# Second attention of a two-layer block: transposes by DMA in place of TensorE, rotations merged, the loop unrolled with twelve steps of lag

## The chip, the cores and the metric

One core of one Trainium2 chip (trn2). The metric is the device time of one execution in microseconds: the median of the runs, lower is better.

## The reference, cut to what matters

The kernel computes four stages on `x` (16 batches, 128 rows, 256 columns): a cosine attention, a ternary feed-forward, a rotary attention with grouped heads and a second ternary feed-forward. The change is in the third:

```python
q = (draft_hidden @ Wq.T).reshape(bsz, draft_len, H, HD)
q = _rms_norm(q, q_norm_w).transpose(0, 2, 1, 3)
kv_in = jnp.concatenate([context_hidden, draft_hidden], axis=1)
k = (kv_in @ Wk.T).reshape(bsz, total_len, KVH, HD)
v = (kv_in @ Wv.T).reshape(bsz, total_len, KVH, HD).transpose(0, 2, 1, 3)
k = _rms_norm(k, k_norm_w).transpose(0, 2, 1, 3)
q = _rope(q, draft_position_ids)
k = _rope(k, full_position_ids)
scores = jnp.einsum('bhqd,bhkd->bhqk', q, k) * SCALE
probs = jax.nn.softmax(scores, axis=-1)
attn = jnp.einsum('bhqk,bhkd->bhqd', probs, v)
attn = attn.transpose(0, 2, 1, 3).reshape(bsz, draft_len, H * HD)
return attn @ Wo.T
```

H is 16 heads of HD 128 elements, KVH 4 key and value heads, each repeated for 4 query heads. Its input is the layer norm of `x`, its keys and values come from 128 context rows and the 128 rows themselves, and its result is added to `x`.

## The kernel before

The program has five parts one behind the other, with a barrier of all engines between them: preparation of weights, first attention, first feed-forward, second attention (`part_c`), second feed-forward. The feed-forwards are written out step by step and already transpose their quantised rows by DMA from SP (lines 730 and 736: 2 blocks of 128x128, and 8 or 6 blocks).

`part_c` works in 64 units: for each of the 16 batches four groups of heads, each with 4 query heads and one key and value head over 256 keys. All large products are made of f16 halves: a value is split into a high half and a low half (what is left), and three products of halves are summed in f32 (`PASSES`). A unit passes through stages that lie some steps apart (`PROJ` 3, `ROPE` 4, `TURN` 5, `SCORE` 6, `EXPS` 7, `VALUE` 8, `ATTEND` 9, `OUT` 10). In each step every engine does its share of all stages, each for another unit, in the order in which its function has them; semaphores order the engines among each other. The steps run in a hardware loop of 8, with 3 rounds peeled off.

- PE (TensorE), function `tensor`: transposes of the rotated queries and keys in f32 (lines 1510, 1529), once in four units of y (1520), projection of keys and values (1544) and of queries (1557), transposes of the probabilities in f32 (1569, 1579), output projection (1589), scores (1601), probabilities times values (1613).
- ACT (ScalarE), `scalar`: high halves out of PSUM (1310 attention output, 1316 queries, 1322 keys, 1334 values, 1357 and 1362 probabilities), a copy of the keys (1340) and its scaling (1347), the four exponentials with their sums (1301).
- DVE (VectorE), `vector`: low halves, each the value in PSUM less its high half (1395, 1401, 1408, 1427, 1449, 1466), products of queries with cosine and sine (1384), sums of squares by statistics of each head (1433, 1443) and what combines them (1460 to 1486), the maximum of the scores (1480), the bias of the exponentials (1494), the reciprocal of the sums (1455), the residual (1374).
- POOL (GpSimd), `pool`: reciprocal roots by a power (1242), the rotations of queries (1250) and keys (1259, 1264), the tables (1274), the scaling of the probabilities (1285).
- SP, `sync`: loads of rows, tables and context of a batch into double buffers (1206 to 1210), the residual rows and the store (1216).

## Time and profile before

| | |
|---|---|
| median of 3 runs | 954.79 us (951.28 to 956.22) |
| the profiled execution | 956.97 us, its span 955.3 us |
| busy share of the span | PE 83%, DVE 86%, ACT 63%, POOL 63% |
| PE's mean granted clock | 0.951 of full speed |
| mean rate of the DMA queues | 56 GB/s |

The span is the time from the first to the last instruction of one execution. An engine's busy time leaves out waits on semaphores and the issuing of DMAs. The chain of waits follows, from the end backwards, what each piece of work was released by. A granted clock of 1.00 is 2.4 GHz, 0.50 is 1.2 GHz.

### The profile page before, as it was taken

Reading aid. Unit: us, or ns where it says so; the run is one execution under the profiler, and the core shown is the slowest. Engines: PE = TensorE matmul, PEld = TensorE weight load, DVE = VectorE, ACT = ScalarE, POOL = GpSimd, SP = SyncE. Lnnn points to the kernel's source line nnn. Section 1 sums busy time; section 2 is a strip of 40 time slices with the busy share of each in tenths; the row PEclk is TensorE's granted clock in tenths of the full one; section 3 lists DMA queues with packets and bytes.
Section 4 is the critical chain, followed back from the end, with each engine's and each line's share of the span. In section 5 each row is a group of like instructions: output and inputs, shape, how many; then the busy total and the mean of one; then the engine's idle time right before and its main releaser. Section 6 shows DMA issues by size and latency. Waiting matters only on the chain.

```text
span 955.3 us, 20235 instructions
## 1 busy us (share of the span) xinstructions
PE 791.0 (83%) x5555; PEld 525.2 (55%) x5555; DVE 817.1 (86%) x2370; ACT 600.0 (63%) x1452; POOL 597.6 (63%) x987
## 2 busy tenths in 40 slices
PE   0285988985575679999999999999999999984776
PEld 0152333331233357777777777777777777653443
DVE  7766799865895689999999999999999999854996
ACT  1565778762794267666667776666667776652552
POOL 1500111122563699999999999899899899831453
PEclk9995999997897899999999999999999999998997
DMA  8204355441244000000000000000000000000245
GB/s 297 102 8 130 118 158 156 144 132 39 46 96 96 29 23 7 29 12 19 30 30 1 28 27 22 5 27 27 0 27 27 27 0 11 13 12 11 42 100 120
DMA packets 89272, 53.31 MB, mean 56 GB/s; under 512 B 43988, under 2 KB 88438, under 8 KB 88950
## 3 DMA queue, kind: packets, MB, share of 16 engines
q1 hardware_dynamic: 89206, 52.54, 19.2%
q8 instruction: 28, 0.46, 0.2%
q14 instruction: 38, 0.31, 0.1%
HBM read 22.10 MB, written 6.29 MB: 30 GB/s over the span
## 4 chain that ended last, share of the span: by engine, by line
PE 54%; DVE 17%; issue 11%; ACT 6%; POOL 5%; DMA 3%; SPq 1%; POOLq 1%; DVEq 0%; ACTq 0%
PE psum L1589 8%; PE psum L1613 8%; PE psum L1601 7%; PE psum L1557 7%; PE psum L1544 7%; PE psum L514 3%; PE psum L1569 3%; PE psum L1579 3%; PE psum L1510 2%; DVE arena L829 2%; PE psum L500 1%; ACT arena L811 1%; DMA arena<-arena 1%; DVE arena L917 1%; ACT arena L805 1%
## 5 line engine op out<-in xcount | busy, mean ns | idle before, releaser
L1301 ACT ACTIVATE arena<-psum,arena 128x256 f32<-128x256 f32 x256 | 147.0, 589 | 2.8 <-DVE arena L1494 2.8
L1285 POOL TENSOR_SCALAR arena<-arena 128x256 f32<-128x256 f32 x256 | 124.2, 485 | 38.5 <-DVE arena L1455 17.1
L1310 ACT ACTIVATE arena<-psum 128x512 f16<-128x512 f32 x64 | 38.2, 597 | 161.6 <-PE psum L1613 161.6
L1557 PE MATMUL psum<-wq_t,arena 128*128 128x512 f16 x384 | 94.6, 383 | 5.0 <-DVE arena L1384 4.6
L1589 PE MATMUL psum<-wo_t,arena 128*128 128x256 f16 x768 | 95.6, 275 | 3.0 <-DVE arena L1395 2.8
L1601 PE MATMUL psum<-arena 128*128 128x256 f16 x768 | 94.4, 273 | 2.8 <-ACT arena L1301 2.7
L1544 PE MATMUL psum<-wkv_t,arena 128*128 128x256 f16 x768 | 95.6, 275 | 0.9 <-DVE arena L1421 0.9
L1613 PE MATMUL psum<-arena 128*128 128x512 f16 x384 | 93.3, 379 | 0.0
L1242 POOL TENSOR_TENSOR arena<-arena,minus_half 128x6 f32<-128x6 f32 x64 | 85.2, 1331 | 10.6 <-DVE arena L1486 7.0
L1250 POOL TENSOR_TENSOR arena<-arena 128x256 f32<-128x256 f32 x128 | 90.6, 729 | 0.3 <-DVE arena L1384 0.3
L342 POOL TENSOR_TENSOR arena<-arena 128x256 f32<-128x256 f32 x16 | 12.0, 747 | 119.3 <-DVE arena L421 119.3
L1259 POOL TENSOR_TENSOR arena<-arena 128x256 f32<-128x256 f32 x128 | 79.4, 642 | 9.6 <-ACT arena L1347 8.4
L1384 DVE TENSOR_TENSOR arena<-psum,arena 128x512 f32<-128x512 f32 x128 | 82.0, 680 | 1.1 <-issue 1.1
L1589 PEld LDWEIGHTS psum<-wo_t,arena 128*128 128x128 f16 x768 | 75.5, 99 | 12.7 <-DVE arena L1395 4.2
L1601 PEld LDWEIGHTS psum<-arena 128*128 128x128 f16 x768 | 75.0, 98 | 12.9 <-issue 3.9
L1480 DVE TENSOR_REDUCE arena<-psum 128x4 f32<-128x1024 f32 x64 | 78.1, 1220 | 4.5 <-PE psum L1601 4.0
L1544 PEld LDWEIGHTS psum<-wkv_t,arena 128*128 128x128 f16 x768 | 75.5, 99 | 10.1 <-DVE arena L1421 1.3
L357 ACT ACTIVATE arena<-psum 128x1024 f32<-128x1024 f32 x64 | 65.1, 1019 | 19.6 <-PE psum L483 19.3
L514 PE MATMUL psum<-arena 128*32 128x256 f32 x512 | 71.4, 402 | 1.9 <-ACT arena L357 1.7
L1449 DVE TENSOR_TENSOR arena<-psum,arena 128x512 f16<-128x512 f32 x64 | 44.2, 691 | 23.4 <-ACT arena L1357 21.7
L1264 POOL TENSOR_TENSOR arena<-arena 128x128 f32<-128x128 f32 x128 | 55.7, 457 | 6.5
L1301 ACT ACTIVATION_READ_ACCUMULATOR arena<-psum,arena 128x1 f32 x256 | 59.0, 230 | 0.0
(201 smaller groups left out, 2006.5 us busy)
## 6 DMA issues: line engine op xcount, KB each, us to landing
arena<-split_scratch SPq DMA_DIRECT2D x96, 64.0 KB, 2.7
arena<-in_x SPq DMA_DIRECT2D x32, 128.0 KB, 2.2
split_scratch<-arena SPq DMA_DIRECT2D x32, 128.0 KB, 1.8
x_rows<-arena SPq DMA_DIRECT2D x32, 128.0 KB, 2.0
arena<-x_rows SPq DMA_DIRECT2D x32, 128.0 KB, 2.0
arena<-in_L_ffn_w SPq DMA_DIRECT2D x2, 1024.0 KB, 6.9
x_rows<-in_L_xattn_Wq SPq DMA_DIRECT2D x1, 2048.0 KB, 13.6
ctx_t<-in_L_xattn_Wo SPq DMA_DIRECT2D x1, 2048.0 KB, 11.7
```

Source lines behind the costliest of these rows:

```text
L514: mm = eng.matmul(value_bank(vp)[r:r + 32, half:half + D], v_t[:, vb.lane % 4, k, h, :], probs[:, q, j, k, :], start=(k == 0), stop=(k == 1))
L1242: eng.tensor_tensor(r[:, lane, :], ms[:, t, :], c.minus_half[:, 0:6], ALU.pow).then_inc(S["r"], 1)
L1250: eng.tensor_tensor(q_rot[:, t, :, s, :], q_cos[:, t, :, s, :], q_sin[:, t, :, 1 - s, :], ALU.add)\
L1259: eng.tensor_tensor(to[:, :, :, :], k_n[:, :, :, :], table["k"][:, wb.lane, :, :, :], ALU.mult)\
L1285: eng.tensor_scalar(probs[:, t, h, :], probs[:, t, h, :], share[:, t, h:h + 1], P_SCALE, ALU.mult, ALU.mult).then_inc(S["probs"], 1)
L1301: eng.activation(probs[:, t, h, :], S_BANKS[:, h, :], ACT.Exp, bias=bias[:, t, h:h + 1], scale=r[:, w.lane % 4, h:h + 1], accum_out=total[ ...
L1384: eng.tensor_tensor(to[:, t, :, :, :].rearrange("p h s f -> p h (s f)"), q_view.rearrange("p h s f -> p h (s f)"), table["q"][:, wb.lane, ...
L1544: mm = eng.matmul(KV_BANK[:, KEYS * row:KEYS * row + KEYS], x_t[:, p, s, k, :], c.wkv_t[:, m, k, g, :, :].rearrange("p a d -> p (a d)"), s ...
L1557: mm = eng.matmul(Q_BANK, y_t[:, p, s, k, :], c.wq_t[:, m, k, SHARE * P * g:SHARE * P * g + SHARE * P], start=(n == 0), stop=(n == 5))
L1589: mm = eng.matmul(O_BANK, a_t[:, t, s, P * h:P * h + P], c.wo_t[:, m, SHARE * g + h, :], start=(g == 0 and h == 0 and n == 0), stop=(g == ...
L1601: mm = eng.matmul(S_BANKS[:, h, :], q_t[:, t, s, P * h:P * h + P], k_t[:, t, m, :], start=(n == 0), stop=(n == 2))
L1613: mm = eng.matmul(A_BANK, v[:, w.lane % 8, s, k, :], p_t[:, t, m, k, :], start=(n == 0), stop=(n == 5))
```

## The change

In `part_c` alone (and `norm_cos` and `norm_sin` become two views of one tensor):

- The loop is written out: 76 steps (`STEPS = TOTAL + LAST`), stages at `ROWS` 1, `HALVES` 2, `PROJ` 4, `ROPE` 5, `TURN` 6, `SCORE` 8, `PROBS` 9, `ATTEND` 10, `OUT` 11, `LAST` 12.
- PE transposes nothing. The rotated queries and keys, y, and the probabilities are split into f16 halves in row layout in SBUF, and SP's DMA transposes turn them: one of 12 blocks (queries and keys), two of 8 (high and low half of the probabilities) per unit, one of 4 (y) per batch.
- The low halves are now made from operands in SBUF.
- POOL writes the high half of the probabilities straight from its scaling, as f16, and DVE writes the low half for each of the four heads.
- Sums of squares: six squares with a sum on ACT in place of six statistics and four small instructions on DVE; the reciprocal root is a logarithm and an exponential on ACT in place of a power on POOL.
- The products with cosine and sine are one instruction for both, on DVE (queries) and POOL (keys); the rotated sum of both halves is one instruction with a swapped view; the tables one instead of two.
- The copy of the keys goes; they are scaled out of PSUM. The projections' banks are doubled.
- Rows, context and tables are read where they lie; the loads, the reload of the residual and the store go.

```diff
-    PROJ, ROPE, TURN, SCORE, EXPS, VALUE, ATTEND, OUT = 3, 4, 5, 6, 7, 8, 9, 10
-    LAST = OUT + 1
+    ROWS, HALVES, PROJ, ROPE, TURN, SCORE, PROBS, ATTEND, OUT, LAST = 1, 2, 4, 5, 6, 8, 9, 10, 11, 12
+    STEPS = TOTAL + LAST
...
     def sync(eng):
+        for s in range(STEPS + 1):
+            b = batch(s, HALVES)
...
+                eng.dma_start_transpose(y_t[:, b % 2, :, :, :].rearrange("p s k r -> p (s k) r"),
+                                        y_hl[:, :, :].rearrange("p s n -> p (s n)")).then_inc(y_turned[b % 2], 16)
+            u = unit(s, PROBS)
+            if u is not None:
+                eng.wait_ge(S["p_hi"], SHARE * (u + 1))
+                wait(eng, S["attn"], u - 1)
+                for half in range(2):
+                    if half:
+                        eng.wait_ge(S["p_lo"], u + 1)
+                    eng.dma_start_transpose(p_t[:, u % 2, half, :, :, :].rearrange("p h k r -> p (h k) r"),
+                                            p_hl[:, u % 2, half, :, :].rearrange("p h k -> p (h k)"))\
+                       .then_inc(p_turned[u % 2], 16)
+            u = unit(s, TURN)
+            if u is not None:
+                eng.wait_ge(S["q_lo"], u + 1)
+                eng.wait_ge(S["k_lo"], u + 1)
+                wait(eng, S["scores"], 2 * (u - 1))
+                eng.dma_start_transpose(qk_t[:, u % 2, :, :], qk_hl[:, u % 2, :]).then_inc(qk_turned[u % 2], 16)
     def pool(eng):
...
+                eng.wait_ge(S["q_cs"], u + 1)
+                wait(eng, S["q_lo"], u - 1)
+                eng.tensor_tensor(straight(q_rot[:, u % 2, :, :]), straight(q_cs[:, 0, :, :]), swapped(q_cs[:, 1, :, :]),
+                                  ALU.add).then_inc(S["q_rot"], 1)
...
+                eng.wait_ge(S["k_n"], u + 1)
+                wait(eng, S["k_rot"], u)
+                eng.tensor_tensor(k_cs[:, :, :, :].rearrange("p t n d -> p t (n d)"),
+                                  k_n[:, :, :].rearrange("p n d -> p (n d)").unsqueeze(1).broadcast_to([P, 2, KEYS]),
+                                  turn["k"][:, b % 2, :, :, :].rearrange("p t n d -> p t (n d)"), ALU.mult)\
+                   .then_inc(S["k_cs"], 1)
...
+            u = unit(s, SCORE)
+            if u is not None:
+                eng.wait_ge(S["share"], 2 * (u + 1))
+                wait(eng, p_turned[u % 2], 32 * (u // 2))
                 for h in range(SHARE):
-                    eng.tensor_scalar(probs[:, t, h, :], probs[:, t, h, :], share[:, t, h:h + 1], P_SCALE,
-                                      ALU.mult, ALU.mult).then_inc(S["probs"], 1)
+                    eng.tensor_scalar(p_hl[:, u % 2, 0, h, :], probs[:, u % 2, h, :], share[:, u % 2, h:h + 1], None,
+                                      ALU.mult).then_inc(S["p_hi"], 1)
     def scalar(eng):
...
+            u = unit(s, SCORE)
+            if u is not None:
+                eng.wait_ge(S["bias"], u + 1)
...
+                for h in range(SHARE):
+                    eng.activation(probs[:, u % 2, h, :], S_BANKS[:, h, :], ACT.Exp, bias=bias[:, u % 2, h:h + 1],
+                                   scale=r[:, u % 8, h:h + 1], accum_out=total[:, u % 2, h:h + 1])\
+                       .then_inc(S["exps"], 1)
+            u = unit(s, PROJ)
+            if u is not None:
...
+                for n in range(2):
+                    eng.activation(junk[:, SHARE + n, :], kv_bank(u)[:, n, 0, :], ACT.Square,
+                                   accum_out=sums[:, u % 2, SHARE + n:SHARE + n + 1])
+            u = unit(s, ATTEND)
+            if u is not None:
+                eng.wait_ge(S["attn"], u + 1)
+                wait(eng, S["o"], u - 1)
+                eng.activation(a_t[:, u % 2, 0, :], A_BANK, ACT.Copy, scale=A_SCALE).then_inc(S["a_hi"], 1)
+            u = unit(s, PROJ)
+            if u is not None:
+                eng.wait_ge(S["q_cs"], u + 1)
+                for h in range(SHARE):
+                    last = eng.activation(junk[:, h, :], q_bank(u)[:, P * h:P * h + P], ACT.Square,
+                                          accum_out=sums[:, u % 2, h:h + 1])
+                last.then_inc(S["ss"], 1)
     def vector(eng):
+        for s in range(STEPS + 1):
+            u = unit(s, OUT)
+            if u is not None:
+                eng.wait_ge(S["a_hi"], u + 1)
+                eng.scalar_tensor_tensor(a_t[:, u % 2, 1, :], A_BANK, A_SCALE, a_t[:, u % 2, 0, :], ALU.mult,
+                                         ALU.subtract).then_inc(S["a_lo"], 1)
+            u = unit(s, PROBS)
+            if u is not None:
+                for h in range(SHARE):
+                    eng.wait_ge(S["p_hi"], SHARE * u + h + 1)
+                    last = eng.scalar_tensor_tensor(p_hl[:, u % 2, 1, h, :], probs[:, u % 2, h, :],
+                                                    share[:, u % 2, h:h + 1], p_hl[:, u % 2, 0, h, :],
+                                                    ALU.mult, ALU.subtract)
+                last.then_inc(S["p_lo"], 1)
+            u = unit(s, SCORE)
+            if u is not None:
+                eng.wait_ge(S["scores"], 2 * (u + 1))
+                wait(eng, S["bias"], u - 1)
+                eng.tensor_reduce(top[:, u % 2, :], S_BANKS, AX.X, ALU.max).then_inc(S["top"], 1)
+            u = unit(s, TURN)
+            if u is not None:
+                eng.wait_ge(S["q_hi"], u + 1)
+                eng.tensor_tensor(q_hl(u, 1), q_rot[:, u % 2, :, :].rearrange("p h d -> p (h d)"), q_hl(u, 0),
+                                  ALU.subtract).then_inc(S["q_lo"], 1)
...
+            u = unit(s, PROJ)
+            if u is not None:
...
+                eng.tensor_tensor(
+                    q_cs[:, :, :, :],
+                    q_bank(u).rearrange("p (h d) -> p h d", h=SHARE).unsqueeze(1).broadcast_to([P, 2, SHARE, HEAD_DIM]),
+                    turn["q"][:, b % 2, :, :].unsqueeze(2).broadcast_to([P, 2, SHARE, HEAD_DIM]), ALU.mult)\
+                   .then_inc(S["q_cs"], 1)
```

The order in a step of `scalar` is: high halves of queries and keys (`TURN`), logarithm and exponential of the sums, high half of the values, the two scaled keys (`ROPE`), once per batch what y needs, four exponentials (`SCORE`), two squares of the keys (`PROJ`), the high half of the output (`ATTEND`), four squares of the queries (`PROJ`). That of `vector`: low half of the output (`OUT`), four low halves of the probabilities (`PROBS`), the maximum (`SCORE`), the low half of the queries (`TURN`), the bias (`SCORE`), the low half of the keys (`TURN`), the merged products of the queries (`PROJ`), the residual once per batch, the scaled sums of the exponentials once all four are there (`SCORE`), the low half of the values (`ROPE`), their reciprocal, and once per batch statistics, y and its low half. That of `pool`: query rotation, key products, key rotation (`ROPE`), a table, four scalings (`SCORE`). That of `tensor`: scores, projections, probabilities times values, output projection.

## Rows read from the trace of the kernel before

**Rows 1.** Timeline of SP at the start of the second attention (start us, us).

```profile
307.64 0.52 SPq L1206 DMA_DIRECT2D arena<-x_rows  x1
```

**Rows 2.** Chain of waits (start us, us, what), in order of time.

```profile
314.86 2.74 PE psum L1544 x12
...
396.10 1.42 PE psum L1557 x6
...
501.32 0.44 PE psum L1510 x4
...
501.98 1.31 PE psum L1544 x12
...
505.02 0.44 PE psum L1579 x4
...
792.81 1.38 PE psum L1557 x6
...
871.47 1.96 DMA x_rows<-arena
```

**Rows 3.** Busy us by stretch: length, PE, PEld, DVE, ACT, POOL, clock, DMA share, GB/s.

```profile
400.00:730.80 330.80, 329.78 (x2506) 251.21 (x2504) 318.44 (x904) 228.82 (x690) 301.54 (x512) 1.00 0.06 21
244.40:298.90 54.50, 36.74 (x206) 18.06 (x204) 48.99 (x195) 51.88 (x65) 33.29 (x44) 1.00 0.44 85
299.00:319.40 20.40, 11.30 (x45) 6.29 (x46) 5.52 (x18) 2.33 (x4) 4.89 (x9) 0.50 0.29 78
```

**Rows 4.** Groups by line and form: xcount | busy us, mean ns | idle before.

```profile
L1285 POOL TENSOR_SCALAR arena<-arena 128x256 f32<-128x256 f32 x256 | 124.2, 485 | 38.5 <-DVE arena L1455 17.1
L1250 POOL TENSOR_TENSOR arena<-arena 128x256 f32<-128x256 f32 x128 | 90.6, 729 | 0.3 <-DVE arena L1384 0.3
L1259 POOL TENSOR_TENSOR arena<-arena 128x256 f32<-128x256 f32 x128 | 79.4, 642 | 9.6 <-ACT arena L1347 8.4
L1480 DVE TENSOR_REDUCE arena<-psum 128x4 f32<-128x1024 f32 x64 | 78.1, 1220 | 4.5 <-PE psum L1601 4.0
L1395 DVE SCALAR_TENSOR_TENSOR arena<-psum,arena 128x512 f16<-128x512 f32 x64 | 43.4, 678 | 6.7 <-ACT arena L1310 6.7
L1374 DVE SCALAR_TENSOR_TENSOR arena<-psum,arena 128x256 f32<-128x256 f32 x16 | 6.6, 414 | 1.6 <-PE psum L1589 1.6
```

**Rows 5.** Timeline of ACT: two exponentials and their accumulator reads.

```profile
504.79 0.60 ACT L1301 ACTIVATE arena<-psum,arena 128x256 f32<-128x256 f32 x1
505.24 0.24 ACT L1301 ACTIVATION_READ_ACCUMULATOR arena<-psum,arena 128x1 f32 x1
505.33 0.61 ACT L1301 ACTIVATE arena<-psum,arena 128x256 f32<-128x256 f32 x1
```

**Rows 6.** Timeline in the first feed-forward: a transpose of 8 blocks, and its reader.

```profile
261.28 1.30 SPq L736 DMA_TRANSPOSE arena<-arena  x1
...
264.41 1.05 PE L954 MATMUL psum<-t_b,arena 128*128 128x256 f16 x8 [0.47 <-DMA arena<-arena]
```

**Rows 7.** DMA rate from 261 to 264.5 us in 40 slices of 0.0875 us.

```profile
GB/s 0 0 35 152 222 205 111 23 0 0 1 0 0 0 0 0 0 50 190 228 219 214 222 214 219 205 214 187 219 196 188 170 59 3 0 0 0 0 0 0
```

**Rows 8.** Timeline of DVE and POOL in three places of the kernel.

```profile
106.60 0.68 DVE L450 TENSOR_TENSOR arena<-arena 128x512 f16<-128x512 f32 x1
106.78 1.09 POOL L345 TENSOR_TENSOR arena<-arena 128x256 f32<-128x256 f32 x1
...
150.79 0.73 POOL L345 TENSOR_TENSOR arena<-arena 128x256 f32<-128x256 f32 x1 [1.31 <-DMA arena<-in_x]
150.82 1.25 DVE L466 SCALAR_TENSOR_TENSOR arena<-arena 128x512 f32<-128x512 f32 x1
...
416.72 2.20 POOL L1285 TENSOR_SCALAR arena<-arena 128x256 f32<-128x256 f32 x4
417.18 0.16 DVE L1470 SCALAR_TENSOR_TENSOR arena<-arena 128x12 f32<-128x12 f32 x1
417.37 0.41 DVE L1475 TENSOR_TENSOR arena<-arena 128x6 f32<-128x6 f32 x1
```

**Rows 9.** One line of DVE: duration ns min/median/max, first and last start.

```profile
L1475 DVE TENSOR_TENSOR arena<-arena x64: 166/167/412, 321.3 to 830.1; 128x6 f32<-128x6 f32 x64
```

More of the change, by code:

```diff
@@ L1188, in part_c @@
+    q_head = lambda u, s, h: qk_t[:, u % 2, SHARE * s + h, :]
+    k_keys = lambda u, s: qk_t[:, u % 2, 2 * SHARE + 2 * s:2 * SHARE + 2 * s + 2, :].rearrange("p n k -> p (n k)")
     S = {n: c.sem("c_" + n) for n in (
[L1189 to L1192 removed]
@@ new lines, in part_c, with unit @@
+        "eps", "stats", "rstd", "y", "y_hi", "y_lo", "tables", "q", "kv", "ss", "r", "q_cs", "q_rot", "k_n", "k_cs",
+        "k_rot", "v_hi", "v_lo", "q_hi", "q_lo", "k_hi", "k_lo", "scores", "top", "bias", "exps", "share", "p_hi",
+        "p_lo", "attn", "a_hi", "a_lo", "o", "out")}
+    y_turned = [c.sem(f"c_y_turned{p}") for p in range(2)]
+    qk_turned = [c.sem(f"c_qk_turned{p}") for p in range(2)]
+    p_turned = [c.sem(f"c_p_turned{p}") for p in range(2)]
+    def unit(s, lag):
+        u = s - lag
+        return u if 0 <= u < TOTAL else None
@@ new lines, in batch @@
+    def batch(s, lag):
+        u = s - lag
+        return u // GROUPS if 0 <= u < TOTAL and u % GROUPS == 0 else None
+    def sync(eng):
+        for s in range(STEPS + 1):
+            b = batch(s, HALVES)
+            if b is not None:
+                eng.wait_ge(S["y_lo"], b + 1)
+                wait(eng, S["q"], GROUPS * (b - 1))
+                eng.dma_start_transpose(y_t[:, b % 2, :, :, :].rearrange("p s k r -> p (s k) r"),
[16 more added lines that the diff above has]
+                eng.dma_start_transpose(qk_t[:, u % 2, :, :], qk_hl[:, u % 2, :]).then_inc(qk_turned[u % 2], 16)
@@ new lines, in tensor @@
+        for s in range(STEPS + 1):
+            u = unit(s, SCORE)
+            if u is not None:
+                eng.wait_ge(qk_turned[u % 2], 16 * (u // 2 + 1))
+                for h in range(SHARE):
+                    if u and h % 2 == 0:
+                        eng.wait_ge(S["exps"], SHARE * (u - 1) + h + 2)
+                    for n, (q, k) in enumerate(PASSES):
+                        mm = eng.matmul(S_BANKS[:, h, :], q_head(u, q, h), k_keys(u, k), start=(n == 0), stop=(n == 2))
+                    if h % 2:
+                        mm.then_inc(S["scores"], 1)
+            u = unit(s, PROJ)
+            if u is not None:
+                b, g = u // GROUPS, u % GROUPS
+                if g == 0:
+                    eng.wait_ge(y_turned[b % 2], 16 * (b // 2 + 1))
+                wait(eng, S["q_cs"], u - 1)
+                wait(eng, S["ss"], u - 1)
+                n = 0
+                for k in range(2):
+                    for x, w in PASSES:
+                        mm = eng.matmul(q_bank(u), y_t[:, b % 2, x, k, :],
+                                        c.wq_t[:, w, k, SHARE * P * g:SHARE * P * g + SHARE * P],
+                                        start=(n == 0), stop=(n == 5))
+                        n += 1
+                mm.then_inc(S["q"], 1)
+                wait(eng, S["k_n"], u - 1)
+                wait(eng, S["v_lo"], u - 1)
+                for row in range(2):
@@ L1571, in body @@
-            w = u.lag(VALUE)
-            if w.live:
-                t = w.lane % 2
-                wait(eng, S["kt_low"], u.lag(TURN).count(1, 1) if u.lag(TURN).live else TOTAL)
-                wait(eng, S["yt_low"], u.of(GROUPS).count(1, 1 if u.lane % GROUPS >= 2 else 0)
-                     if u.live else BATCHES)
-                wait(eng, S["pt_b_low"], w.count(1))
-                for h in range(SHARE):
-                    mm = eng.transpose(TB[:, P * h:P * h + P], probs[:, t, h, P:2 * P], c.ident[:, :])
-                mm.then_inc(S["pt_b"], 1)
@@ L1581, in body @@
-            w = u.lag(OUT)
-            if w.live:
-                t, b, g = w.lane % 2, w.of(GROUPS), w.lane % GROUPS
-                wait(eng, S["at_low"], w.count(1, 1))
-                if g == 0:
-                    wait(eng, S["out"], b.count(1))
-                for h in range(SHARE):
-                    for n, (s, m) in enumerate(PASSES):
-                        mm = eng.matmul(O_BANK, a_t[:, t, s, P * h:P * h + P], c.wo_t[:, m, SHARE * g + h, :],
+                mm.then_inc(S["attn"], 1)
@@ L1590, in body @@
+            u = unit(s, OUT)
+            if u is not None:
+                b, g = u // GROUPS, u % GROUPS
+                eng.wait_ge(S["a_lo"], u + 1)
+                if g == 0:
+                    wait(eng, S["out"], b)
+                for h in range(SHARE):
+                    for n, (a, w) in enumerate(PASSES):
+                        mm = eng.matmul(O_BANK, a_t[:, u % 2, a, P * h:P * h + P], c.wo_t[:, w, SHARE * g + h, :],
                                         start=(g == 0 and h == 0 and n == 0),
```

553 lines of the change are left out of this document (159 added, 394 removed).

## Prediction

> **What bounds the kernel now.** I read the chain of waits first. The second attention runs from its first load at 307.6 us [rows 1] to the landing of its last store at 873.4 us, some 566 us, and in its steady stretch the chain is PE alone, one group of matmuls behind the other [rows 2]. The projection of the queries starts at 396.10 us and, 48 units later, at 792.81 us: 8.27 us a unit. The unit's own pieces show what the change takes from PE: four transposes of f32 queries 0.44 us, twice four of probabilities 0.88, two of keys half of four, 0.22, together 1.54 us (and the rows of y once in four units), beside five groups of some 1.3 us that stay, 8.05 us in all. Then the busy times by stretch: over 330.8 us PE is busy for 329.8, DVE for 318.4, POOL for 301.5, ACT for 228.8 [rows 3]. A unit thus has 8.25 us of PE, 7.96 of DVE, 7.5 of POOL and 5.7 of ACT: three engines are nearly full, so no more than the slack of the fullest can be won unless all three are relieved. The profiled execution took 956.97 us, 1.7 above its span and 2.2 above the median of 954.79.
>
> **The change part by part, per unit.** All engines now go by steps, one unit in each stage per step.
>
> PE loses its transposes: 8.05 less 1.54 leaves 6.5 us.
>
> DVE loses six sums by statistics, two evictions of low halves of probabilities (2 x 0.68) and the chain of small ones. It gets the low halves of the probabilities in row layout, four of 256 elements, at most 0.41 each by the nearest form (L1374) [rows 4]; the low halves of queries and keys from SBUF instead of PSUM, 0.68 and 0.41; one merged cosine and sine product of 1024 elements, taken as 1.22 as the other 1024-element reading of PSUM (L1480) [rows 4], instead of two of 0.68. Instructions overlap by some 0.08. Sum about 6.4 us: lighter.
>
> POOL loses the power of six elements and half of its other instructions. It keeps four scalings of 0.48 (L1285) [rows 4], which the timeline has 0.57 apart (four in 2.20 [rows 8]). The query rotation becomes one sum of 512 elements: between one of today's 256-element forms (0.73) and two (1.46) (L1250) [rows 4]; I take 1.23, since work per element dominates. The two key products become one of 512: 0.64 to 1.28 (L1259) [rows 4], I take 1.10; the key rotation one of 256, 0.70; the tables 0.65 in three steps of four. Sum 5.7 us.
>
> ACT loses the two evictions of transposed probabilities and the copy of the keys, and gets six squares with a sum each, two small activations for the reciprocal root and again four exponentials. An exponential takes 0.45 to its accumulator read and the next starts 0.09 later [rows 5], 0.54 in all; a square of half the elements lies between 0.31 and 0.54, taken as 0.32 as it loads no per-partition scale or bias. With 6 x 0.32 + 4 x 0.54 + the high halves and copies (my estimate from the exponentials' rate, 0.5 for 512 elements and 0.27 for up to 256: 2.1 in all) + 0.5 + 0.2 of per-batch work it has 6.9 us.
>
> The queue: SP issues three transposes a unit (12, 8 and 8 blocks of 128x128) and one of 4 blocks a batch; loads, stores and reloads of rows go. An 8-block one is issued in 1.30 us and its reader starts 3.13 us after the issue began [rows 6]; its data move in some 1.25 us (14 slices of 0.0875 us at about 210 GB/s [rows 7]). Issue: 4 x 1.3 at most, 5.2 us; data: 29 blocks at 0.157, 4.5 us. Both fit beside a step of 6.5 us, and queries and keys have nearly two steps until they are read, probabilities one. SP waits first for the probabilities' halves; the queries' transpose queued behind them has that slack. I cost the DMAs at nothing; the cover is the lag. In the filling they cost some 5 us against two loads and a store that go (2 us each).
>
> So by the engines alone the step would be 6.9 us, ACT's. Two things make it longer.
>
> First, one loop crosses engines within a step. Put 0 where DVE has written the bias of the exponentials. ACT: four exponentials to 2.2, squares of two key rows to 2.85, the high half of the attention's output (0.60) to 3.45. Only then may DVE, which has this first in the next step, write the low half: 0.60, to 4.05 (L1395, less overlap) [rows 4]. Then four low halves of probabilities (1.6), the maximum (1.13), the queries' low half (0.60), the bias (0.15): 7.5 us and round again. That is the step if nothing else intervenes.
>
> Second, what DVE now does in that loop reads two operands of SBUF, and the trace shows what that costs beside POOL. The same DVE instruction of 6 elements that takes 0.167 us in the median took 0.41 [rows 9] while POOL was at its scalings; a 512-element one, 0.68 where it begins first, took 1.25 behind a POOL sum of 0.73 begun 0.03 earlier; and a POOL sum took 1.09 instead of 0.73 when such a DVE instruction had begun 0.18 before it [rows 8]. So each waits for the whole instruction of the other: DVE holds POOL off for 0.18 + 0.36 = 0.54 us per 512 elements, 0.27 per 256. Instructions with one operand in PSUM, nearly all of today's, show none of it: L1374 and L1395 keep 0.41 and 0.68 beside a POOL busy for nine tenths [rows 3, 4]. The Trainium skill (SBUF — State Buffer, Who interferes with whom) says the same of a DVE instruction with two SBUF inputs against a GpSimd one that reads SBUF: the first gets the ports for its whole length. By that rule the walk below holds; if they were shared by bandwidth instead, the sum would be that of rival A, 906 us.
>
> The walk: exponentials summed at 2.35, share ready at 2.95 (DVE writes the values' low half between), POOL's scalings from then; the third ends at 4.60. DVE wants its first low half at 4.2, gets through at 4.60, gives it back at 4.87. Fourth scaling to 5.35, second low half to 5.62, query rotation to 6.85, third to 7.12, key products to 8.22, fourth to 8.49. Maximum from PSUM to 9.55; meanwhile key rotation to 9.2 and the table to 9.85; queries' low half to 10.4, bias 10.5. Without a table 10.2; with POOL's 512-element forms at 1.0, 9.9. I take **10.2 us**, against 8.27. Of this POOL stands still from 9.85 to 2.95 of the next, about 3.6 us.
>
> **Sum.** 60 full steps x 10.2 = 612; four at the end without projections or rotations at 7.5 = 30; filling and draining as today, 566 - 64 x 8.27 = 37. Together 679 for 566: +113 on the profiled 957, less 2 to the median, **1068 us**. Steps of 9.7 to 10.9 give 1038 to 1110.
>
> **Rivals.** A: the loop without port waits, 7.5 us (7.1 to 8.0): 64 x 7.5 + 37 = 517, 49 less, 906 us (880 to 940): faster. For it: three engines are relieved, and a different phase could let POOL's long sums fall beside the maximum and the merged product, which read PSUM. Against it: POOL cannot start its scalings before the share, and its rotations are queued right behind them, where DVE's low halves are. It decides if low halves stay at 0.41. B: POOL's forms are cheap and half of the waits vanish, 8.9 us: 607 for 566, 996 us. C: no change, steps of 8.27. D: the clock. PE would be busy for 6.5 of 10.2 us, with some 3 us idle in each step. Today it is never idle in this part and its clock stays at 1.00, 2.4 GHz; in the first feed-forward, busy for 67%, it also stayed at 1.00 for 54 us, then fell to 0.50, 1.2 GHz, for the next 20 [rows 3], where a group of 12 matmuls takes 2.74 us instead of 1.31 [rows 2]. A low step costs PE about 13 us; with half of the steps low, 32 x 3 us more, about 1165. E: the transposes by DMA are twice as slow as measured and the queue bounds at 9 to 10 us: same sum as the forecast by another way; the rows speak against it, and I give it nothing of its own.
>
> **How the numbers follow.** Forecast 0.58; clock on top of it 0.12; B 0.09; no change 0.05; A 0.16. Slower by over 0.5% (about what a measurement of this kernel can tell from no change): 0.79, within it 0.05, faster 0.16. The range has to take in the case of the other sign in part: from 935, which leaves out two thirds of A (0.11), to 1145, which leaves out half of the clock's (0.06). The forecast's own range is 1038 to 1110.
>
> **What would show it.** Right: the low halves of probabilities at 0.6 to 1.3 us mean in place of 0.41, the queries' low half above 0.7, the chain changing between DVE, POOL and ACT with PE under 65% busy, a step of 10 us, SP waiting for semaphores. Wrong: low halves of 0.41 and a chain of ACT and DVE alone (A), PE's matmuls of 0.2 us in long stretches (D), PE waiting for landings of DMA (E).

## The result, and the profile after

The changed kernel takes 1095.82 us (median of 4 runs, 1093.26 to 1097.89) against 954.37 of the kernel before beside it: ratio 1.148 with a 95% interval of 1.144 to 1.152. It is 15% slower. The forecast was 1068, with 1038 to 1110 as its own range. Ratios below leave out an execution that is more than 1.5% above its kernel's fastest, while medians keep it: there are two, 926.10 us of the kernel with both edits and 1066.53 us (mean granted clock 0.66) of the one with the waits and the two-operation scalings.

The page of the profiled execution (1097.03 us, its span 1095.3): busy time of each engine, share of the span, instructions; then the chain that ended last, by engine and by line.

```profile
PE 764.6 (70%) x4627; PEld 441.2 (40%) x4627; DVE 876.7 (80%) x1842; ACT 649.5 (59%) x2188; POOL 632.4 (58%) x669
...
POOL 39%; issue 31%; DVE 13%; PE 9%; ACT 4%; DMA 3%; SPq 1%; POOLq 1%; DVEq 0%; ACTq 0%
POOL arena L1278 15%; POOL arena L1250 8%; POOL arena L1244 7%; POOL arena L1266 4%; POOL arena L1256 3%; PE psum L514 3%; DVE arena L829 2%; DMA arena<-arena 1%; PE psum L500 1%; DVE arena L917 1%; ACT arena L811 1%; ACT arena L805 1%; PE psum L483 1%; DVE arena L584 1%; POOL arena L574 1%
```

PE, which alone made the chain of the second attention before [rows 2], has gone from it there; POOL's five kinds of instructions in the second attention are in its place. The chain alone would mislead, though. Between 400 and 900 us it holds nothing but POOL and 40% "issue", and the long pieces of "issue" are POOL's own idle time before its scalings, which the waits below give to DVE's share. By itself it cannot tell whether POOL's work or the loop through DVE and ACT sets the step; the experiments do. No engine is full any more. Busy times in 500 us of the steady stretch, which answer to [rows 3] (length, PE, PEld, DVE, ACT, POOL, clock, DMA share, GB/s):

```profile
400.00:900.00 500.00, 365.18 (x2260) 231.20 (x2261) 423.57 (x675) 307.94 (x1358) 383.96 (x367) 0.90 0.49 92
```

Before, PE was busy for all of its stretch; now it is for 73%, DVE for 85% with its port waits counted as busy, POOL for 77%. The step, taken from one start of the bias on DVE (L1389) to the next, is 10.51 to 10.60 us, 10.55 on average from the fifth to the 60th, against 8.25 before. At the very end, where POOL has scalings but no rotations, two steps last 8.31.

The groups, by line and form, which answer to [rows 4] (xcount | busy us, mean ns | idle before):

```profile
L1278 POOL TENSOR_SCALAR arena<-arena 128x256 f16<-128x256 f32 x256 | 233.8, 930 | 162.0 <-DVE arena L1426 162.0
L1370 DVE SCALAR_TENSOR_TENSOR arena<-arena 128x256 f16<-128x256 f32 x256 | 223.6, 874 | 42.8 <-POOL arena L1278 42.5
L1250 POOL TENSOR_TENSOR arena<-arena 128x512 f32<-128x512 f32 x64 | 92.1, 1440 | 5.4 <-ACT arena L1309 5.4
L1244 POOL TENSOR_TENSOR arena<-arena 128x512 f32<-128x512 f32 x64 | 81.5, 1273 | 7.9 <-DVE arena L1402 7.9
L1256 POOL TENSOR_TENSOR arena<-arena 128x256 f32<-128x256 f32 x64 | 70.1, 1095 | 5.0
L1382 DVE TENSOR_TENSOR arena<-arena 128x512 f16<-128x512 f32 x64 | 44.8, 700 | 1.7 <-ACT arena L1289 1.7
L1389 DVE SCALAR_TENSOR_TENSOR arena<-arena 128x4 f32<-128x4 f32 x64 | 42.0, 656 | 0.1
```

Two things stand out. DVE's low half of the probabilities (L1370) takes 0.87 us on average where the forecast's row has 0.41, and the bias, four elements, takes 0.66. (The kernel with PSUM operands below gives their own lengths, 0.48 and 0.15.) And POOL's scaling (L1278) takes 0.93 us where the kernel before had 0.485 for the same 256 elements. The timeline of DVE and POOL in one step shows where each of them lies (start us, us, what, idle before and its releaser):

```profile
499.81 0.17 DVE L1426 RECIPROCAL arena<-arena 128x4 f32<-128x4 f32 x1
500.08 3.62 POOL L1278 TENSOR_SCALAR arena<-arena 128x256 f16<-128x256 f32 x4 [2.13 <-DVE arena L1426]
...
501.04 0.69 DVE L1370 SCALAR_TENSOR_TENSOR arena<-arena 128x256 f16<-128x256 f32 x1
...
503.67 1.27 POOL L1244 TENSOR_TENSOR arena<-arena 128x512 f32<-128x512 f32 x1
...
503.74 1.48 DVE L1370 SCALAR_TENSOR_TENSOR arena<-arena 128x256 f16<-128x256 f32 x1 [0.21 <-POOL arena L1278]
...
504.89 1.45 POOL L1250 TENSOR_TENSOR arena<-arena 128x512 f32<-128x512 f32 x1
505.14 1.21 DVE L1378 TENSOR_REDUCE arena<-psum 128x4 f32<-128x1024 f32 x1
...
506.28 0.67 DVE L1382 TENSOR_TENSOR arena<-arena 128x512 f16<-128x512 f32 x1
506.43 1.11 POOL L1256 TENSOR_TENSOR arena<-arena 128x256 f32<-128x256 f32 x1
506.88 0.68 DVE L1389 SCALAR_TENSOR_TENSOR arena<-arena 128x4 f32<-128x4 f32 x1
...
507.59 0.57 ACT L1333 ACTIVATE arena<-psum,arena 128x256 f32<-128x256 f32 x1 [4.14 <-DVE arena L1389]
```

The share is ready, and POOL scales for 3.62 us. The query rotation follows at 503.67, 0.07 us ahead of the fourth low half, which ends 0.28 us after it. The key rotation starts at 506.43 beside the queries' low half, and the bias ends at 507.56, 0.02 after it. Only then do the exponentials begin. The waits of the 500 us say the same (who waited, for whom: us in total, times, longest):

```profile
ACT arena L1333 <- DVE arena L1389: 192.0, 48, 4.2
POOL arena L1278 <- DVE arena L1426: 111.2, 47, 3.1
...
PE psum L1458 <- ACT arena L1333: 84.4, 53, 3.5
...
PE psum L1496 <- DMA arena<-arena: 35.1, 12, 4.4
```

and in SP's queue

```profile
SPq L1212 <- DVE arena L1444: 143.5, 12, 12.0
```

ACT waits 4 us in each step for the bias, POOL some 2.4 for the share, PE for the exponentials. The row of the DMA has 12 waits of PE for the probabilities' transposes. The last row shows what is behind them: once per batch SP stands for up to 12 us at the normed rows' transpose (L1212), whose low half DVE writes last in its step, and the probabilities' transposes are queued behind it.

### The profile page after: what moved, and what is told of

Its sections match the earlier page's. It is cut to its first block, busy times and chain, and to the rows that moved or that the text cites. A ratio compares the mean times of both kernels' runs of the same rounds, so it can differ in the third digit from the quotient of the medians.

```text
span 1095.3 us, 17060 instructions
## 1 busy us (share of the span) xinstructions
PE 764.6 (70%) x4627; PEld 441.2 (40%) x4627; DVE 876.7 (80%) x1842; ACT 649.5 (59%) x2188; POOL 632.4 (58%) x669
## 4 chain that ended last, share of the span: by engine, by line
POOL 39%; issue 31%; DVE 13%; PE 9%; ACT 4%; DMA 3%; SPq 1%; POOLq 1%; DVEq 0%; ACTq 0%
POOL arena L1278 15%; POOL arena L1250 8%; POOL arena L1244 7%; POOL arena L1266 4%; POOL arena L1256 3%; PE psum L514 3%; DVE arena L829 2%; DMA arena<-arena 1%; PE psum L500 1%; DVE arena L917 1%; ACT arena L811 1%; ACT arena L805 1%; PE psum L483 1%; DVE arena L584 1%; POOL arena L574 1%
## 5 line engine op out<-in xcount | busy, mean ns | idle before, releaser
L1278 POOL TENSOR_SCALAR arena<-arena 128x256 f16<-128x256 f32 x256 | 233.8, 930 | 162.0 <-DVE arena L1426 162.0
L1370 DVE SCALAR_TENSOR_TENSOR arena<-arena 128x256 f16<-128x256 f32 x256 | 223.6, 874 | 42.8 <-POOL arena L1278 42.5
L1458 PEld LDWEIGHTS psum<-arena 128*128 128x128 f16 x768 | 80.2, 113 | 163.2 <-issue 123.6
L1250 POOL TENSOR_TENSOR arena<-arena 128x512 f32<-128x512 f32 x64 | 92.1, 1440 | 5.4 <-ACT arena L1309 5.4
L1244 POOL TENSOR_TENSOR arena<-arena 128x512 f32<-128x512 f32 x64 | 81.5, 1273 | 7.9 <-DVE arena L1402 7.9
L1402 DVE TENSOR_TENSOR arena<-psum,arena 128x1024 f32<-128x1024 f32 x64 | 77.5, 1212 | 7.9 <-PE psum L1471 7.9
L342 POOL TENSOR_TENSOR arena<-arena 128x256 f32<-128x256 f32 x16 | 11.9, 746 | 121.3 <-DVE arena L421 121.3
L1256 POOL TENSOR_TENSOR arena<-arena 128x256 f32<-128x256 f32 x64 | 70.1, 1095 | 5.0
L1496 PEld LDWEIGHTS psum<-arena 128*128 128x128 f16 x384 | 37.3, 101 | 86.1 <-DMA arena<-arena 50.8
L1355 ACT ACTIVATE arena<-psum 128x128 f32<-128x128 f32 x256 | 69.2, 318 | 3.4 <-DVE arena L1402 3.4
L1471 PEld LDWEIGHTS psum<-wq_t,arena 128*128 128x128 f16 x384 | 44.5, 116 | 55.5 <-issue 31.8
L1355 ACT ACTIVATION_READ_ACCUMULATOR arena<-psum 128x1 f32 x256 | 63.7, 251 | 0.0
L1364 DVE SCALAR_TENSOR_TENSOR arena<-psum,arena 128x512 f16<-128x512 f32 x64 | 44.0, 687 | 17.9 <-ACT arena L1349 14.4
```

What stands on the lines that cost most here:

```text
L1244: eng.tensor_tensor(straight(q_rot[:, u % 2, :, :]), straight(q_cs[:, 0, :, :]), swapped(q_cs[:, 1, :, :]), ALU.add).then_inc(S["q_rot"], 1)
L1250: eng.tensor_tensor(k_cs[:, :, :, :].rearrange("p t n d -> p t (n d)"), k_n[:, :, :].rearrange("p n d -> p (n d)").unsqueeze(1).broadcast_ ...
L1256: eng.tensor_tensor(straight(k_rot[:, u % 2, :, :]), straight(k_cs[:, 0, :, :]), swapped(k_cs[:, 1, :, :]), ALU.add).then_inc(S["k_rot"], 1)
L1278: eng.tensor_scalar(p_hl[:, u % 2, 0, h, :], probs[:, u % 2, h, :], share[:, u % 2, h:h + 1], None, ALU.mult).then_inc(S["p_hi"], 1)
L1355: last = eng.activation(junk[:, h, :], q_bank(u)[:, P * h:P * h + P], ACT.Square, accum_out=sums[:, u % 2, h:h + 1])
L1370: last = eng.scalar_tensor_tensor(p_hl[:, u % 2, 1, h, :], probs[:, u % 2, h, :], share[:, u % 2, h:h + 1], p_hl[:, u % 2, 0, h, :], ALU.m ...
```

## The experiments

Theory 1 is the forecast's: POOL's instructions and DVE's with two SBUF operands hold each other up on the loop bias, exponentials, share, scalings, low halves, maximum, bias. The scalings at 0.92 us are a loss of their own beside it. Theory 2: the slow scalings, or POOL's sum of work, alone. Theory 3, in the first experiment: the 0.92 belong to the f16 output and not to the form. Step lengths are those of the profiled execution of each kernel, taken as above, on average from the fifth to the 60th. The diffs are shortened: [...] and ... stand for what is left out, and the comments are not in the kernels.

**Two-operation scalings.** The share is multiplied in, and then 1.0.

```diff
-eng.tensor_scalar(p_hl[...], probs[...], share[...], None, ALU.mult)
+eng.tensor_scalar(p_hl[...], probs[...], share[...], 1.0, ALU.mult, ALU.mult)
```

> The changed kernel, whose four scalings on POOL multiply by the share and then by 1.0 (two operations in one instruction, as the kernel before had it) instead of by the share alone. The changed kernel's step is 10.55 us and its scalings take 922 ns each, where the two-operation form of the kernel before took 482 ns. Theory 1 (the step is set by port waits between POOL and DVE's instructions with two SBUF operands, on the loop through the exponentials; the one-operation form is a second, separate loss): scalings fall to about 0.48 and four take 2.2 instead of 3.6 us, but the low halves of the probabilities, which now run beside them, are pushed behind them, so only part of the 1.4 us comes back: step 9.9 to 10.2, 1055 to 1075 us. Theory 2 (the slow scalings alone are what the step has over the forecast loop, port waits are minor): all of it comes back, step 9.15, about 1010 us. Theory 3 (the duration belongs to the f16 output, not to the form): scalings stay at 0.92, no change.

1039.48 us, ratio to the kernel before 1.087 (1.078 to 1.096); step 9.70.

```profile
498.15 2.00 POOL L1278 TENSOR_SCALAR arena<-arena 128x256 f16<-128x256 f32 x4 [4.26 <-DVE arena L1426]
499.08 4.17 DVE L1370 SCALAR_TENSOR_TENSOR arena<-arena 128x256 f16<-128x256 f32 x4
500.12 1.43 POOL L1244 TENSOR_TENSOR arena<-arena 128x512 f32<-128x512 f32 x1
501.58 1.38 POOL L1250 TENSOR_TENSOR arena<-arena 128x512 f32<-128x512 f32 x1
```

In the step shown four scalings take 2.00 us instead of 3.62. The output is f16 as before, so the form made the 0.92; theory 3 falls. The changed kernel itself has the same answer in its feed-forwards, where a scaling with two operations also writes f16 from f32:

```profile
L768 POOL TENSOR_SCALAR arena<-arena 128x256 f16<-128x256 f32 x32 | 16.1, 503 | 13.6 <-DVE arena L882 13.6
```

Over 56 steps the four scalings take 2.16 us instead of 3.65, 1.5 less, and the step gets 0.85 of it. The low halves now run beside them and are pushed behind POOL's rotations: the third behind the query rotation and the fourth behind the key products in the step shown (4.17 us for the four), only the fourth in about half of the steps (3.1 to 3.2). From the first scaling's start to the last low half's end it is 4.56 us instead of 5.17, and the bias meets the key rotation in 27 of the 56 steps instead of in all. That is theory 1's mechanism, but neither theory's number: the gain is above theory 1's bounds (0.35 and 0.65) and well under what theory 2 expected (1.4).

**Low halves and bias with an operand in PSUM.**

```diff
-q_bank = lambda u: c.bank(u % 2)
+q_bank = lambda u: c.bank(0)
+zeros = c.bank(1)[:, 0:256]
 ...
-eng.scalar_tensor_tensor(p_hl[...], probs[...], share[...], ...)
+eng.scalar_tensor_tensor(p_hl[...], zeros, share[...], ...)
```

and likewise for the low halves of queries and keys and for the bias. (Those of the values and of the attention's output read PSUM in the changed kernel too.)

> The changed kernel, whose low halves of the probabilities, queries and keys and whose bias take their first operand from a PSUM bank of zeros instead of from SBUF, so that DVE has no instruction of part C's loop with two large SBUF operands; the bank is won by giving the query projections one bank instead of two. The result is another one (low halves are minus the high ones, the maximum is left out of the exponentials); the number of instructions and their sizes stay. Theory 1 (port waits): the fourth low half takes 0.5 to 0.6 instead of 1.48 us, the bias 0.16 instead of 0.68, the queries' low half 0.6; the loop shortens by 1.0 to 1.3 us, step 9.3 to 9.5, 1020 to 1035 us, while POOL's rotations keep their length or lose a little of it. Theory 2 (slow scalings alone): no change, step 10.4 to 10.6, within 1% of 1096 us.

1003.08 us, ratio 1.049 (1.040 to 1.058); step 9.02. The low halves are now made from zeros, so this kernel's result is another one; only its time counts. Theory 2 falls: POOL does the same work, DVE the same number of instructions of the same size, and the step is 1.53 us shorter, more than the 1.0 to 1.3 that theory 1 expected. The groups:

```profile
L1278 POOL TENSOR_SCALAR arena<-arena 128x256 f16<-128x256 f32 x256 | 234.3, 932 | 112.8 <-DVE arena L1431 112.8
L1374 DVE SCALAR_TENSOR_TENSOR arena<-psum,arena 128x256 f16<-128x256 f32 x256 | 123.6, 483 | 81.3 <-POOL arena L1278 80.8
L1250 POOL TENSOR_TENSOR arena<-arena 128x512 f32<-128x512 f32 x64 | 81.1, 1268 | 4.8 <-ACT arena L1309 4.8
...
L1256 POOL TENSOR_TENSOR arena<-arena 128x256 f32<-128x256 f32 x64 | 46.9, 733 | 5.0
...
L1394 DVE SCALAR_TENSOR_TENSOR arena<-psum,arena 128x4 f32<-128x4 f32 x64 | 9.7, 152 | 0.1
```

Low halves of 0.48, a bias of 0.15, key products of 1.27 instead of 1.44, a key rotation of 0.73 instead of 1.10; the scalings stay at 0.93, so their length is no port wait. These are the forms' own lengths. (PE now waits 38.5 of 400 us for its one bank of queries. That it costs nothing is not shown.)

**Both edits together.** 

> Both edits of the two kernels before it: two-operation scalings on POOL, and zeros in PSUM as first operand of the low halves and the bias (the result is another one). Theory 1: nothing pushes the low halves behind the shorter scalings any more, so the two gains add up: 10.55 - 1.4 - 1.2 = 7.9 to 8.3 us a step, 935 to 965 us, about the kernel before. Theory 2: as with two-operation scalings alone, 9.15, about 1010 us. Theory 3 (scalings stay at 0.92): as with the PSUM operands alone.

916.95 us, ratio 0.959 (0.948 to 0.971); the step is 7.42 in three of four and 7.67 on average. This is faster than theory 1 expected (7.9 to 8.3, 935 to 965 us). The gain over the changed kernel is 2.88 us a step, more than the 0.85 and 1.53 of the two alone: the scalings are the short ones (1.87 us for four), and the low halves beside them keep their 0.47. The 7.42 is close to the forecast's loop without port waits, 7.5. With two-operation scalings, operands in SBUF in place of PSUM thus cost 9.70 less 7.67, 2.0 us a step.

**The query rotation moved** into the time of the exponentials, behind the table and ahead of the scalings, with its waits.

```diff
-u = unit(s, ROPE)   # q_rot first of the step
+u = unit(s, PROJ)   # q_rot behind the table, ahead of the scalings
```

> The changed kernel with POOL's query rotation moved: it is issued after the table of the step before and ahead of the scalings, in the 3 us in which POOL waits for the share while the exponentials run. Nothing is added or left out. Theory 1 (port waits on the loop): the key products now come directly behind the scalings and block the fourth low half of the probabilities in its place, but the key rotation is over before the bias: the bias falls from 0.68 to 0.16 us and the step by 0.3 to 0.5, to 10.1 to 10.2, about 1070 us. Theory 2 (POOL's own chain of work sets the step): the 1.27 us of the rotation leave the chain, step 9.3, about 1020 us. Theory 3 (neither): no change.

1086.71 us, ratio 1.136 (1.127 to 1.145); step 10.40, a gain of 0.15 where theory 1 expected 0.3 to 0.5. The intervals of the two times just meet; the steps tell them apart. Its timeline:

```profile
500.41 1.27 POOL L1272 TENSOR_TENSOR arena<-arena 128x512 f32<-128x512 f32 x1 [2.17 <-DVE arena L1404]
501.22 0.47 DVE L1419 TENSOR_SCALAR arena<-arena 128x4 f32<-128x4 f32 x1 [0.56 <-ACT arena L1335]
...
505.80 1.27 POOL L1246 TENSOR_TENSOR arena<-arena 128x512 f32<-128x512 f32 x1
505.87 1.48 DVE L1372 SCALAR_TENSOR_TENSOR arena<-arena 128x256 f16<-128x256 f32 x1 [0.21 <-POOL arena L1280]
```

The bias fell to 0.15 as expected, and the key products took the rotation's place in front of the fourth low half, which kept its 1.48. But the first instruction of the share, four elements, was now held until the rotation ended (0.47 instead of 0.17), and the share came 0.3 later. Here, moving POOL's work into a gap only moved the collision. Theory 2 (9.3) is excluded again.

**Two waits added on POOL**, and nothing else.

```diff
+wait(eng, S["p_lo"], min(s - PROBS, TOTAL - 1) + 1)   # ahead of the query rotation
+wait(eng, S["k_lo"], u)                               # ahead of the key products
```

> The changed kernel with two waits added on POOL and nothing else: the query rotation waits for the low halves of the probabilities of the step, and the key products wait for the low half of the keys that follows the bias on DVE. POOL's big instructions so lie beside DVE's maximum (PSUM operand) and beside the exponentials, not beside DVE's instructions with two SBUF operands. POOL still does all of its work, only later. Theory 1 (port waits on the loop through the exponentials): the fourth low half falls from 1.48 to 0.5 to 0.7 us, the bias from 0.68 to 0.15, the step to what the kernel with PSUM operands had, 9.0 to 9.4 us, about 1000 to 1025 us, although waits were only added. Theory 2 (POOL's own sum of work sets the step): its 9.6 us of work in 10.55 can't shrink and two waits are added, so 10.5 us or more, 1096 us or slower.

1018.52 us, ratio 1.070 (1.064 to 1.077); step 9.29, 1.26 shorter than without the waits. The result and all the work are those of the changed kernel. Its timeline:

```profile
508.92 0.48 DVE L1372 SCALAR_TENSOR_TENSOR arena<-arena 128x256 f16<-128x256 f32 x1 [0.21 <-POOL arena L1280]
509.32 1.22 DVE L1380 TENSOR_REDUCE arena<-psum 128x4 f32<-128x1024 f32 x1
509.49 1.26 POOL L1245 TENSOR_TENSOR arena<-arena 128x512 f32<-128x512 f32 x1 [0.60 <-DVE arena L1372]
510.46 0.84 DVE L1384 TENSOR_TENSOR arena<-arena 128x512 f16<-128x512 f32 x1
511.23 0.15 DVE L1391 SCALAR_TENSOR_TENSOR arena<-arena 128x4 f32<-128x4 f32 x1
```

POOL stands idle for 0.60 us so that the fourth low half can go at 0.48, and its rotation then lies beside the maximum, which reads PSUM. The bias is back at 0.15; the queries' low half, which meets the rotation's end, pays with 0.84 instead of 0.70. Step and time are within what theory 1 expected. This is the cleanest evidence for theory 1: waits were only added, and the kernel became 7% faster.

**SyncE's order.** The normed rows' transposing DMA last in its step instead of first.

> The changed kernel with SyncE's queue in another order: the transposing DMA of a batch's normed rows is issued after the probabilities' and the queries' and keys' of its step instead of ahead of them. In the changed kernel PE waits at the attention products for the probabilities' transposes behind it, 12 times in the 500 us from 400 on, 35.1 us together and up to 4.4 us at a time. Theory 1 (DVE, POOL and the exponentials set the step): PE has the slack, no change within 0.5%, step 10.55 us. Theory 4 (the DMA transposes and their queue hold the step): up to 35 of 500 us come back, 1050 to 1060 us.

1091.20 us, ratio 1.143 (1.138 to 1.148) against 1.148 (1.144 to 1.152): the intervals overlap; step 10.55, as before. The queue does not hold the changed kernel.

**The waits and the two-operation scalings together**, first with all scalings on POOL, then with the fourth head's high half made by ACT:

```diff
-for h in range(SHARE):            # POOL
+for h in range(3):
+eng.activation(p_hl[:, u % 2, 0, 3, :], probs[:, u % 2, 3, :], ACT.Copy, scale=share[:, u % 2, 3:4])   # ACT
```

> The two added waits on POOL together with the two-operation scalings. Theory 1: behind the last scaling only the rest of the low halves (about 1.0 us), the maximum 1.21, the queries' low half 0.6 and the bias stand before the exponentials: step 7.8 to 8.2 us, 930 to 950 us, level with the kernel before or 1 to 2% under it, with the right result. Theory 2 (POOL's sum of work, now about 7.0 us, with the waits on DVE as idle time around it): 9.0 us or more, 1005 us.

> As the kernel with the added waits and two-operation scalings, and ACT makes the high half of the fourth head of the probabilities (a copy with the share as its scale, ahead of its squares of the queries) while POOL makes the other three. Theory 1: POOL is through 0.5 us earlier, ACT has that time free, the low halves end some 0.4 us earlier: step 7.4 to 7.8 us, 900 to 925 us. Rival: PE, whose own work is 6.5 us a step and more in its low-clock stretches, or ACT becomes what the step waits for, and nothing is gained over the kernel without it.

959.21 us, ratio 1.004 (1.001 to 1.008), and 967.85, ratio 1.012 (1.004 to 1.019). Both miss what theory 1 expected, the second by more. In the first three steps of four were as short as expected, 8.1 us; in the second they took 7.8 to 7.9, just above the expected 7.4 to 7.8. Every fourth, the one in which a batch's rows are turned, took up to 10.8 in the first kernel and up to 10.9 in the second, there 10.5 in the median. In the first kernel, over 400 us:

```profile
PE psum L1498 <- DMA arena<-arena: 42.1, 11, 4.6
...
DVE arena L1380 <- PE psum L1460: 8.8, 9, 1.4
```

PE waits up to 4.6 us for the probabilities' transposes, and DVE's maximum now waits for PE. SP stands at the normed rows' transpose for up to 9.7 us. The same late DMA was there in the changed kernel (4.4 us), where a step of 10.55 hid it.

**Both with SyncE's new order.**

> The added waits on POOL with two-operation scalings, all four scalings on POOL, and SyncE's queue with the normed rows' transposing DMA last in its step. Without the new order three steps of four take 8.1 us and the fourth 8.2 to 10.8. Theory 1 with the queue as the next bound: all steps 8.1 us, 60 times 0.3 less than 959 us: 938 to 945 us. Rival: the fourth step keeps its length, 955 to 960 us.

> Two edits already run, together: the added waits on POOL with two-operation scalings and ACT making the fourth head's high half, and SyncE's queue with the normed rows' transposing DMA issued last in its step. In the kernel without the new order three steps of four take 7.8 to 7.9 us and every fourth about 10.5: PE waits 4.2 us at the attention products for the probabilities' transposes, ACT and DVE wait for PE. Theory 1 with the queue as the next bound (a late transpose that the long step of the changed kernel hid is in the open once the step is short): every fourth step falls to about 7.9, 15 times 2.6 us less, 925 to 935 us, under the kernel before by 2 to 3%. Rival (the fourth step is long for another reason, the normalisation's extra instructions on DVE and ACT): it keeps 10 us or more, 960 to 970 us.

With four scalings on POOL 941.15 us, ratio 0.984 (0.978 to 0.990), step 8.11; with ACT's head 928.00 us, ratio 0.971 (0.965 to 0.977), step 7.91. Both are within what was expected. None of the 56 steps is over 8.32 us any more, PE has no such wait for a transpose left, SP's longest at the normed rows' transpose is 1.6 us (with four scalings on POOL), and the edit that was worth nothing at a step of 10.55 is worth 2 to 4% here.

**The low half of the attention's output later** on DVE, behind the keys' low half, in the kernel of 928.00 us.

> As the kernel with ACT's head and the new order of SyncE's queue, and DVE subtracts the attention output's low half behind the keys' low half, under the exponentials, instead of ahead of the low halves of the probabilities. Theory 1: the low halves, the maximum and the bias come up to 0.3 or 0.4 us earlier and the step falls to 7.5 us, 905 to 915 us. Rival (PE's order: its attention and output products then wait for the later half and push the next scores back by as much): no gain, or up to 1 us a step more, 930 to 990 us.

921.64 us, ratio 0.962 (0.957 to 0.967), step 7.75, between the two expectations. The interval overlaps that of the kernel without it. Waits over 400 us:

```profile
PE psum L1505 <- DVE arena L1403: 52.7, 51, 1.2
ACT arena L1336 <- DVE arena L1393: 42.2, 51, 1.2
DVE arena L1374 <- POOL arena L1281: 20.4, 40, 0.7
```

PE's attention products now wait 1 us a step for the low half that was moved, but there is no row of a wait for PE, so the rival is not what holds the step. POOL's scalings are: the share is ready 2.94 us behind the bias as before, so the first low half, free to come 0.4 earlier, finds its scaling not done (last row). It starts at 3.55 instead of 3.97, and four take 2.1 us beside three scalings instead of 1.9. In the three steps of four with a table POOL comes 0.1 later still, and they take 7.73 to 7.89 us on average instead of 7.62. This kernel has the lowest median of those that compute the reference's result: 3.8% under the kernel before and 16% under the changed one (0.962 / 1.148 = 0.838).

## Why the prediction was right, and where not

- **What bounds it.** Right in kind: the low halves of the probabilities took 0.87 (0.6 to 1.3), and ACT, POOL and DVE wait for each other in a circle. The chain did not show it as forecast: PE fell out of it, but it is POOL's and "issue", not one of DVE, POOL and ACT. PE was busy for 73%, not under 65%: 7.7 us a step, where it needs 6.7 in the kernel with both edits at a clock of 1.00 throughout (forecast 6.5), the rest fits its spells at 1.2 GHz (mean clock 0.90). The queries' low half, at 0.70, was just at its mark.
- **The step,** 10.55 for 10.2, and that it came so close is partly luck: two errors nearly cancelled. The scalings were costed at 0.48 from a row [rows 4] whose instruction has two operations; the changed line has one and takes 0.92, 1.4 us more for four. The walk let each low half wait for a whole POOL instruction; beside the slow scalings each lost only 0.21 us (0.69 instead of 0.48), so three of them were through when the fourth scaling ended, and only the fourth met a rotation. The walk's other terms held: the first scaling starts 3.05 us after the bias ended (2.95), the maximum ends at 9.3 (9.55), the bias at 10.5 without a table and 10.6 with one (10.2 and 10.5). The key rotation against the bias, 0.5 us, was not in the walk; it came since the key rotation lay later than thought. The test without that luck is the kernel with two-operation scalings, which are the ones the walk counted: its step is 9.70 for the walk's 10.2, its time 1039.48 us for 1068, and its port waits are 2.0 us a step for 2.7 (10.2 less 7.5). So the term was there and the right way, and about a third too large.
- **The unit costs.** From the kernel with PSUM operands: query rotation 1.27 (1.23), key products 1.27 (1.10), key rotation 0.73 (0.70), table 0.73 (0.65), forecast a little low. An exponential took 0.54 in all, as forecast, the merged product 1.21 (1.22), a square 0.25 (0.32). With 7.42 the loop without port waits is near the forecast's 7.5.
- **The sum.** 28 us over the forecast: 60 times 0.35 are 21. The steps at the end took 8.31 instead of 7.5, since their scalings are the slow ones, and the drain has a wait of 4.6 us for a transpose. How the last 7 us divide among these was not taken apart.
- **DMA at nothing.** Right for this kernel, as SyncE's new order shows, and right for its reason: the lag covered it. That rules out rival E too, although its sign, PE waiting for landings, was there. What the forecast left out is that SP stands at the normed rows' transpose, up to 12 us, ahead of the probabilities'; it looked only at what was queued behind those. The cover has a limit: at steps of 7.9 to 8.1 us the normed rows' transpose in front of the probabilities' was worth 18 us with four scalings on POOL (959.21 to 941.15) and 40 with ACT's head (967.85 to 928.00).
- **Rival A**, no port waits, is what the kernel with both edits shows to be possible (916.95 us, forecast 906), not what the change does. Its condition, that POOL's long sums fall beside the maximum and the exponentials, needed two waits. **B** was half there: of the walk's two waits, behind the query rotation and behind the key products, one did not come. But POOL's forms were not cheap, the scalings above all, and the bias got a wait that nobody had counted, so the step was not 8.9.
- **Rival D**, the clock. It did fall: granted 0.90 in the mean of the stretch, at 0.50 (1.2 GHz) for a part of 32 of the 56 steady steps. Those steps are 10.56 us long and the other 24 10.54, so it cost nothing here. The rival took PE's work at the low clock as 13 us over a whole step; the spells cover at most 0.65 of a step, and PE's other slack took them up. In the faster kernels it starts to count. With ACT's head and the new order all 8 steps with a spell are fourth steps, and they take 8.18 us; the other six fourth steps take 7.85. In six of the 8 DVE's maximum waits 0.4 to 0.6 us for PE's scores, in the others it does not wait.

## What to carry to other kernels

Before work moves from PSUM to SBUF, list for each DVE instruction whether all its tensor operands will be in SBUF, and what POOL does in the same stretch; where both meet on a loop, choose the order so that POOL's long instructions fall beside DVE's PSUM readers, with an added wait if need be. Take a duration from a row of the same form, number of operations included, and measure the form alone where there is none. When a stretch gets faster, look again at the waits that the slow version hid: an edit worth nothing before may be worth 4% now.

## What the runs showed that was not expected

- On POOL a scaling of 256 f32 elements to f16 takes 0.92 to 0.93 us with one operation and 0.48 with two, the second of which multiplies by 1.0. It keeps 0.93 in the kernel with PSUM operands, where no DVE instruction that runs beside it in every step has two operands in SBUF, so it is the form's own. Why was not found.
- The whole-instruction wait is not general. DVE's low half behind a POOL rotation ends 0.28 us after it; beside a one-operation scaling, 0.92 us long, it ends 0.17 us before the scaling does (501.73 against 501.90), having lost 0.21. The rule cited from the Trainium skill (SBUF — State Buffer, Who interferes with whom) is borne out by the first and does not cover the second.
- An instruction with one tensor operand, in SBUF, of four elements (the share's first) also waited for the end of a rotation: 0.47 us instead of 0.17. The forecast had counted instructions with two SBUF operands only. The same section of the Trainium skill also names DVE's tensor_scalar among those that can take the shared ports, which this row bears out.
